# The queries' cosine product reads the SBUF copy, later in VectorE's order, and tile 4's scores are parted 320 and 320

## The reference, cut to what matters

```python
q = rope(einsum('bim,mhd->bhid', x, wq))      # rope: [even*cos - odd*sin, even*sin + odd*cos]
k = rope(einsum('bim,mhd->bhid', x, wk))
s = einsum('bhid,bhjd->bhij', q, k) / 128     # causal: j <= i
o = einsum('bhij,bhjd->bhid', softmax(s), v)
x = layernorm(x + einsum('bhid,hdm->bim', o, wo))
```

## Time and profile before

| what | value |
|---|---|
| runs | 1764.21, 1767.45, 1772.24 us |
| median | 1767.45 us |
| profiled execution | 1769.15 us, of which the span is 1767.3 us |
| PE busy | 1694.9 us (96%) |
| DVE busy | 1431.5 us (81%) |
| ACT busy | 1237.6 us (70%) |
| POOL busy | 1134.0 us (64%) |
| granted TensorE clock, mean | 0.99 |

### The profile page before, as it was taken

How to read it: one execution, slowest core, us unless ns; L and a number is a source line. 1 busy time by engine, 2 the same in 40 slices (tenths; PEclk the granted TensorE clock), 3 DMA queues, 4 the chain that set the end, 5 groups by cost and what they waited for, 6 DMA issues and landing times. The chain is left out here.

```text
span 1767.3 us, 33370 instructions
## 1 busy us (share of the span) xinstructions
PE 1694.9 (96%) x10524; PEld 1481.7 (84%) x10524; DVE 1431.5 (81%) x2945; ACT 1237.6 (70%) x2361; POOL 1134.0 (64%) x684
## 2 busy tenths in 40 slices
PE   5999999999999999999999999999999997999996
PEld 4788888888888888888888888888888886889886
DVE  4888988897889888977898889879889887677764
ACT  3777777776777777767777777777777763665663
POOL 4566666665666656666666666666666654677775
PEclk9999999999999999999999999999999999999999
DMA  4222232223222322232223222322232323123212
GB/s 143 65 61 77 73 101 61 76 73 86 66 74 73 100 67 73 73 97 73 73 73 96 73 73 73 96 73 72 72 85 72 85 73 93 46 62 94 60 31 54
DMA packets 76518, 134.23 MB, mean 76 GB/s; under 512 B 19264, under 2 KB 45888, under 8 KB 76352
## 3 DMA queue, kind: packets, MB, share of 16 engines
q1 hardware_dynamic: 74880, 130.10, 27.7%
q10 hardware_dynamic: 1472, 2.10, 0.4%
HBM read 56.36 MB, written 8.70 MB: 37 GB/s over the span
## 5 line engine op out<-in xcount | busy, mean ns | idle before, releaser
L493 ACT ACTIVATE probs<-ps_slot,neg_max 128x640 f32<-128x640 f32 (+7 forms) x512 | 378.7, 741 | 121.1 <-DVE neg_max L600 111.7
L600 DVE CUSTOM_DVE_ANT_0 ps_slot<-ps_slot,causal 128x640 f32<-128x640 f32 (+7 forms) x512 | 386.8, 756 | 58.1 <-PE ps_slot L57 57.3
L816 PE MATMUL ps_turn<-ident,probs 128*128 128x128 f32 x2304 | 338.8, 277 | 19.8 <-DVE x_t L657 6.3
L426 POOL TENSOR_TENSOR q<-rot_q,q 128x1024 fp32r<-128x1024 f32 x64 | 153.9, 2404 | 245.0 <-ACT q L510 245.0
L816 PEld LDWEIGHTS ps_turn<-ident,probs 128*128 128x128 f32 x2304 | 257.7, 141 | 51.6 <-DVE x_t L657 8.0
L55 PE MATMUL ps_slot<-k,q 128*128 128x512 f32 (+3 forms) x768 | 285.0, 371 | 2.7 <-DVE rot_q L616 1.5
L57 PE MATMUL ps_slot<-k,q 128*128 128x512 f32 (+3 forms) x768 | 267.8, 349 | 0.0
L56 PE MATMUL ps_slot<-k,q 128*128 128x512 f32 (+3 forms) x768 | 267.1, 348 | 0.0
L418 POOL TENSOR_TENSOR swapped_q<-swapped_q,rope 128x1024 f32<-128x1024 f32 x64 | 170.8, 2669 | 77.0 <-DMA swapped_q<-unrot_q 76.9
L426 POOL TENSOR_TENSOR k<-rot_k,k 128x1024 fp32r<-128x1024 f32 x64 | 153.1, 2392 | 82.3 <-ACT k L510 79.8
L527 ACT ACTIVATE pt_split<-ps_turn 128x512 fp32r<-128x512 f32 x256 | 145.2, 595 | 61.8 <-PE ps_turn L816 61.8
(11 more groups left out here) (168 smaller groups left out, 4348.6 us busy)
## 6 DMA issues: line engine op xcount, KB each, us to landing
swapped_k<-unrot_k SPq DMA_DIRECT2D x128, 256.0 KB, 3.6
swapped_q<-unrot_q SPq DMA_DIRECT2D x128, 256.0 KB, 3.7
inv_b<-inv_rows SPq DMA_DIRECT2D x64, 512.0 KB, 5.0
x_rows<-in_L_attn_x SPq DMA_DIRECT2D x8, 512.0 KB, 5.2
y_t<-y_sum SPq DMA_DIRECT2D x8, 512.0 KB, 5.2
x_rows<-y_t SPq DMA_DIRECT2D x8, 512.0 KB, 3.9
unrot_q<-in_L_attn_x SPq DMA_DIRECT2D x8, 512.0 KB, 5.4
row_b<-r_rows SPq DMA_DIRECT2D x16, 256.0 KB, 3.5
```

Of the source, the lines that this page charges most:

```text
L426: pool.tensor_tensor(out[:, 1, :], rot[which][:, :], f32(out[:, 0, :]), ALU.subtract)\
L493: act.activation(probs_tile(t), score_tile(name, head, i), ACT.Exp, scale=-1.0, bias=neg_max[:, head.par, t:t + 1], accum_out=sums[:, head ...
L600: dve.tensor_tensor_reduce(tile, tile, causal[:, T - WIDTH[t]:T], -1.0, UNSEEN, ALU.add, ALU.min, neg_max[:, head.par, t:t + 1]).then_inc( ...
L816: last = pe.transpose(bank[:, at:at + P], probs_tile(t)[:, j * P:(j + 1) * P], ident[:, :])
```

## The change

Four edits:

- `mul_cos_q` reads `unrot_q` (SBUF) in place of the PSUM slot, and moves in DVE's step from the first place to the one between the row maxima of tile 6 and `rotate_add(1, after)`.
- PE's tile 7 no longer waits for `cos_made_q` but for `raw_made_q`, ACT's copy.
- ACT's copy of the next head's queries, and a load into `unrot_q` at the end of the attention, wait for `cos_made_q`, since the product now reads `unrot_q`.
- Tile 4's scores start at column 192 of the slot, so that its 640 columns are parted by the bank's border at 512 into 320 and 320.

```diff
+SLOT_OFFSET = {"s4": 192}
...
-            return slot(name, head)[:, i * BANK:i * BANK + WIDTH[t]]
+            at = i * BANK + SLOT_OFFSET.get(name, 0)
+            return slot(name, head)[:, at:at + WIDTH[t]]
...
                     sp.wait_ge(swap_landed[0], last * 32)
+                    sp.wait_ge(cos_made[0], last)
                     sp.dma_start(kept.x_row, x[0, :, :].rearrange("(t p) m -> p t m", p=P)).then_inc(ahead_landed, 16)
...
                     act.wait_ge(sin_made[which], head.step(-1).made())
+                    act.wait_ge(cos_made[which], head.step(-1).made())
...
-                dve.tensor_tensor(rot[0][:, :], slot("q", head), kept.rope[:, 0, :], ALU.mult).then_inc(cos_made[0], 1)
+                dve.tensor_tensor(rot[0][:, :], unrot[0][:, :], kept.rope[:, 0, :], ALU.mult).then_inc(cos_made[0], 1)
...
-                mul_cos_q(after)
                 invert(before)
...
                 rowmax("s6", head)
+                mul_cos_q(after)
                 rotate_add(1, after)
...
-                    for c0 in range(0, WIDTH[t], BANK):
-                        cols = slice(c0, min(c0 + BANK, WIDTH[t]))
+                    room = BANK - SLOT_OFFSET.get(name, 0)
+                    for cols in (slice(0, min(room, WIDTH[t])), slice(room, WIDTH[t])):
+                        if cols.start >= cols.stop:
+                            continue
...
-                    pe.wait_ge(cos_made[0], head.made())
                     pe.wait_ge(raw_made[0], head.made())
...
-                free_slot(cos_made[0], after)
+                free_slot(raw_made[0], after)
                 scores("s7", head)
```

## The result

The changed kernel takes 1810.27 us (median of 5 runs, 1805.91 to 1812.29) against 1767.45. The ratio is 1.0234, with a 95% interval from 1.0213 to 1.0255: slower by 2.3%. The forecast was 1801 with a range from 1765 to 1830. The profiled execution took 1808.97 us, with a span of 1807.1.

What follows compares the result with a forecast made beforehand. PE's chain was taken as the bound, other engines counting only where PE waits. Longer steps (28.5 us) and swap scatter (5), together 33, on 1767.45 gave 1800.5, say 1801 us; range 1765 to 1830.

Steps and rivals of the forecast that it cites:

- The mechanism: POOL's queries' sine product holds DVE's moved cosine product until 715.69; the keys' addition ends late and PE waits 0.88 us.
- PE's wait at "6b": PE's transposes wait for DVE's low part of "4b": 0.88 us a step, three times as long as before.
- tile 7's wait: PE's wait for the cosine product before tile 7, 0.20 us a step, was to be gone.
- a free port: Faster rival: POOL does not hold DVE's cosine product, so PE's gains come whole; 28 us less, 1739; chance 0.18.
- Tile 4: PE's scores as 320 and 320 columns, spaced 0.147 us: saves 0.10 us a step, 6.4 us over 64 heads.
- A step without scatter: One step of the attention loop, from one copy of the keys to the next: 22.33 us after the change.
- The scatter of the swap: Later landings of the queries' swap delay POOL's product: a quarter of the steps at 0.3 us each, 5 us.
- The margin of 0.64: Time from the queries' swap landing at 712.66 to POOL's end of the keys' sine product at 713.30.
- step A: Step of the kernel before, 22.02 us, where POOL's queries' sine product starts first and holds DVE's keys' addition to 3.40.
- The second rival: Cosine product runs first, then POOL's queries' sine product holds the keys' addition: 64 us more, 1831; chance 0.12.
- The sum: Over the attention loop, 28.5 us from longer steps plus 5 us from late swaps, together 33 us more.

Runs made afterwards that it cites:

- The short sine product: The changed kernel with POOL's sine product of the queries on 128 columns instead of 1024, the rest left out: 1741.43 us, ratio 0.9847.
- the fastest kernel: The changed kernel with POOL's sine product of the queries also waiting for the cosine product, not for the keys' addition: 1750.93 us, ratio 0.99.

## Why the prediction was right, step by step

- **The mechanism** was right in each link: POOL's queries' product back to back with the keys', the cosine product 0.67 behind it (0.63 in the prediction) and held to a mean of 2.81 us (2.8), PE's wait at "6b", tile 7's wait gone. The mean is that good in part by luck: the clean step has 2.81, the steps with a late swap have more, and a few have 1.22. The short sine product, and the full one that waits for the cosine product, show that this one meeting makes the loss (1741 and 1751, against the 1739 worked out for a free port). That a multiplication is held as the addition is, which the prediction could not read from its trace, is now shown: in 56 of the changed kernel's 63 steps the queries' sine product held the cosine product, which ended 1.08 to 1.09 us behind it each time.
- **Tile 4**: 0.147 us for a spacing of 320 columns; measured 0.14 to 0.15, and 0.10 saved a step. That it would bring 6.4 us "if nothing else is late" was harmless in the sum, which let PE wait anyway; alone it brought nothing. The other possibility that the prediction names, that both partings cost the same, did not come true: 1.06 us against 0.96.
- **A step without scatter** was put at 22.33 and is 22.22. The term that was too long is the one between the two DVE instructions: 0.06 was added for the semaphore, and the addition started 0.08 ahead of the product's end in the profile.
- **The scatter of the swap was mis-sized.** It was given 5 us: a quarter of the steps, 0.3 each. The 52 plain steps (without a load of new tokens or a turn of the loop) have a mean of 22.50, 0.28 above the clean one, which is 18 us over 63 steps. The margin of 0.64 was not there: in 33 of the 52 steps, and not in a quarter, POOL starts the queries' product later than the end of the keys', by 0.24 us in the mean over all 52. SP's queue in the step read above, to be held against the earlier trace rows:

```profile
727.02 1.10 SPq L339 DMA_DIRECT2D swapped_k<-unrot_k  x2
728.24 0.53 SPq L346 DMA_DIRECT2D inv_rows<-inv  x1
728.95 1.58 SPq L339 DMA_DIRECT2D swapped_q<-unrot_q  x2
```

  The store takes 0.53 to issue instead of 0.33 and the two swaps 1.58 instead of 1.10, and the swap is issued 3.13 us into the step, not 2.88. Together 0.73 later than the prediction had it (0.25 at the start and 0.48 in the two issues). From its own issue the second swap lands about as fast as in step A (3.65 us, 3.73 there), so the pair is in 7.77 us into the step. POOL could start at 7.94, where the prediction has 712.66 − 705.37 = 7.29. That is 0.65 later and just the end of the keys' product, so any scatter beyond it goes straight into POOL's start. Why the issues are longer where they follow the keys' DMAs so closely is not shown.
- **The second rival** was there in part. In five of the 63 steps the swap landed late enough for the product to slip in first and for the addition to be held. The step at 1162.96, 22.83 us long, on DVE and on POOL:

```profile
1171.57 1.22 DVE L620 TENSOR_TENSOR rot_q<-unrot_q,rope 128x1024 f32<-128x1024 f32 x1
1172.70 3.41 DVE L627 TENSOR_TENSOR rot_k<-rot_k,swapped_k 128x1024 f32<-128x1024 f32 x1
...
1171.80 3.23 POOL L421 TENSOR_TENSOR swapped_q<-swapped_q,rope 128x1024 f32<-128x1024 f32 x1 [0.78 <-DMA swapped_q<-unrot_q]
```

- **The sum.** The two profiled executions differ by 1808.97 − 1769.15 = 39.8 us: 52 plain steps with 22.50 − 21.86 = 0.64 each, 33.4, and about 7 from the steps in which tokens are loaded or the loop turns. The prediction had 33. Two errors cancel in part: the clean step, 0.11 shorter than forecast, is worth 7 us over 63 steps, and the scatter, 18 instead of 5, is worth 13 the other way.

## What to carry to other kernels

Before an operand is moved from PSUM to SBUF on VectorE, count what the instruction then reads: with two SBUF inputs it can meet a GpSimd product, and then its price is no longer its own 1.22 us but the rest of what GpSimd has in hand and 1.08 us more. An earlier signal is neither gain nor loss by itself: the earlier reciprocal alone gave 8 us to the kernel before, and in the changed one it let a GpSimd product start in front of the instruction that mattered. Where two engines meet at such a port in every step, set their order by a semaphore that lets the less urgent one ask just behind the urgent one; and read an experiment step by step, since a total can be the mean of two outcomes, neither of which it resembles.

## What was not expected of the hardware

- The issue time of a DMA on SP's queue is not a constant: the same pair of swaps took 1.10 us where SP had paused 1.7 us between the keys' pair and the store, and 1.58 where pair, store and pair followed each other closely.
- The price of losing the meeting is the same each time. In the ten traces with the whole sine product, a VectorE instruction of 1.22 us with two SBUF inputs that came second to it ended 1.08 to 1.09 us behind it (418 times), and a sine product that came second ended 2.22 to 2.27 us behind the VectorE instruction (180 times). The one exception is a meeting in the kernel before with both starts within 3 ns, which went to VectorE.
- A GpSimd instruction that has been let go by its semaphore and stands before the port loses no time when the port comes free: in the kernel where it asked 0.27 us behind the keys' addition it ended 0.33 earlier in the step than in the one where it waited for the addition's semaphore (13.24 against 13.57 us).
- For two VectorE instructions in a row that both need the port, the port did not change hands between them in the fastest kernel, where GpSimd asked 0.27 us after the second had started; where GpSimd's transfer landed during the first, the second was held for 3.41 us. In these meetings the one that asked first had it each time.
